# Last batch of a two-layer kernel's first attention: its normalization ahead of the next layer's rows, and the pieces woven into that layer's first group moved by one step

## What is computed

```
x = x + L0_xattn(layernorm(x), ctx)     # latent attention, per batch
x = x + L0_ffn(layernorm(x))            # gated feed-forward in 8-bit floats
x = x + L1_xattn(layernorm(x), ctx, ctx)
x = x + L1_ffn(layernorm(x))            # top-2 of 8 experts
# L0_xattn, for one batch
p   = softmax(theta(ctx) @ phi(x))
t_x = p @ g(x)                          # 128 x 512 per batch
h   = relu((t_x - mean(t_x)) * rsqrt(var(t_x) + eps) * gamma + beta)   # mean and var over ALL of t_x
out = out_w @ h + out_b + ctx
# L0_ffn
out = q(gelu(q(x) @ q(w0)) * (q(x) @ q(w1))) @ q(w_linear)
```

## Time and profile before

| | us |
|---|---|
| median of 3 runs (837.96 to 839.0) | 838.62 |
| the profiled execution | 841.42 |
| its span (first to last instruction) | 839.7 |
| busy in the span: PE | 744.5 |
| DVE | 578.2 |
| ACT | 398.3 |
| POOL | 354.9 |

### The profile page before, as it was taken

How to read it: one execution, slowest core, us unless ns; L and a number is a source line. 1 busy time by engine, 2 the same in 40 slices (tenths; PEclk the granted TensorE clock), 3 DMA queues, 4 the chain that set the end, 5 groups by cost and what they waited for, 6 DMA issues and landing times. The chain is left out here.

```text
span 839.7 us, 14278 instructions
## 1 busy us (share of the span) xinstructions
PE 744.5 (89%) x4265; PEld 307.2 (37%) x4265; DVE 578.2 (69%) x1100; ACT 398.3 (47%) x744; POOL 354.9 (42%) x344
## 2 busy tenths in 40 slices
PE   4999997989999999798999899999971699999993
PEld 2344443444444443121222222222231355555551
DVE  4688888585858587668988988976746255555551
ACT  2534543553636372476777667746750222222220
POOL 4654454012020212536576587565465033333332
PEclk9999999999999999799999999968995799999998
DMA  8999740018181775333434453434343589889974
GB/s 307 352 133 257 275 185 0 1 36 303 36 297 71 271 255 183 76 94 84 103 100 103 100 167 94 110 102 119 99 146 142 90 111 131 123 135 120 121 103 62
DMA packets 114166, 117.51 MB, mean 140 GB/s; under 512 B 54824, under 2 KB 78248, under 8 KB 113840
## 3 DMA queue, kind: packets, MB, share of 16 engines
q1 hardware_dynamic: 102992, 94.48, 40.4%
q0 software_dynamic: 10384, 22.02, 15.4%
q10 hardware_dynamic: 720, 0.13, 0.1%
HBM read 43.61 MB, written 59.56 MB: 123 GB/s over the span
## 5 line engine op out<-in xcount | busy, mean ns | idle before, releaser
L1422 ACT ACTIVATE t_room<-l_b 128x512 f32<-128x512 f32 x256 | 139.3, 594 | 53.6 <-PE l_b L1317 47.8
L1930 POOL DMA_INDIRECT out<-ex_y,t_tag x39 | 61.6, 1581 | 123.9 <-DMA out<-ex_y,t_tag 63.7
L1826 PE MATMUL ex_hp<-w1h,h_stack 128*128 x312 | 78.1, 320 | 17.2 <-DVE ex_hl L1879 16.7
L1495 DVE TENSOR_REDUCE l_negm<-l_a 128x2 f32<-128x1024 f32 x64 | 75.2, 1220 | 16.6 <-PE l_a L1262 16.6
L1846 PE MATMUL ex_yp<-w2h,ex_ht 128*128 (+1 forms) x234 | 76.2, 380 | 5.2 <-DVE ex_ht L1890 4.5
L1495 DVE TENSOR_REDUCE h_negm<-l_a 128x2 f32<-128x1024 f32 x56 | 66.0, 1221 | 17.9 <-PE l_a L1262 17.9
L1865 ACT ACTIVATE ex_hf<-ex_pre 128x352 f32<-128x352 f32 x39 | 19.4, 497 | 118.2 <-DVE ex_pre L1885 118.2
L1328 PE MATMUL l_pv<-t_room,l_vt 128*32 128x512 f32 x512 | 73.1, 645 | 0.1
L1336 PE MATMUL l_sm<-t_room,ones_f 128*32 128x512 f32 x512 | 70.3, 623 | 0.0
L806 PE MATMUL ps_st<-f_xt,wg 128*128 128x512 fp8e4 x256 | 65.7, 379 | 3.4 <-ACT f_y L857 1.8
L806 PE MATMUL ps_r<-f_xt,wg 128*128 128x512 fp8e4 x256 | 65.7, 379 | 0.0
(11 more groups left out here) (247 smaller groups left out, 1482.2 us busy)
## 6 DMA issues: line engine op xcount, KB each, us to landing
slots_x<-empty SPq DMA_DIRECT2D x8, 2376.0 KB, 11.1
slots_x<-empty SPq DMA_DIRECT2D x7, 2112.0 KB, 16.1
h_stack<-h_parts SPq DMA_DIRECT2D x96, 64.0 KB
l_stack<-l_parts SPq DMA_DIRECT2D x96, 64.0 KB
f_stage<-in_w SPq DMA_DIRECT2D x8, 704.0 KB, 7.2
w1l<-in_ctx SPq DMA_DIRECT2D x8, 512.0 KB, 8.3
f_stage<-in_w SPq DMA_DIRECT2D x8, 512.0 KB
h_kf<-in_ctx SPq DMA_DIRECT2D x16, 256.0 KB, 3.1
```

The costliest lines, as they stand in the source:

```text
L1422: act.activation(weights_at(u, c, h)[:, :], B[t % 2][:, :], ACT.Exp, scale=SCALE).then_inc(b_ok, 1)
L1495: dve.tensor_reduce(negm[u % 2][:, 2 * half:2 * half + 2, j], A[half][:, :, :], AX.X, ALU.max, negate=True)\
L1826: mm = pe.matmul(HP[i % 2][:, 0:H], xt[i % AHEAD][:, xp * FC + f, :], w1p[wp][:, bass.ds(e, 1), f * H:(f + 1) * H], start=k == 0, stop=k = ...
L1930: pool.indirect_dma_start(out=out, out_offset=bass.IndirectOffsetOnAxis(ap=tags[i % TAGS][:, 0:1].bitcast(U32), axis=0), in_=y[i % YS][:, ...
```

## The change

Two edits, no instruction added or removed.

1. In the last attention step, DVE's `G.normal_rows(dve, X, 0, ...)` moves from ahead of `normalized(dve, 7)` to behind it.
2. In the first feed-forward group, PE's `variance_of(7)` moves from the end of step 3 to step 4, `mean_of(8)` from 10 to 11 and `variance_of(8)` from 12 to 13. DVE's `spread_of(8)` moves from the end of step 9, where it stood behind `added(7)`, to the end of step 8.

```
             if m == 1:
                 pe.wait_ge(sr_ok, B)
                 mean_of(pe, B - 1)
-            if m == 3:
+            if m == 4:
                 variance_of(pe, B - 1)
...
-            if m == 10:
+            if m == 11:
                 mean_of(pe, B)
-            if m == 12:
+            if m == 13:
                 variance_of(pe, B)
...
                 if more:
                     normal_rows(i + 1)
-                else:
-                    G.normal_rows(dve, X, 0, range(G.G))
                 if back:
                     normalized(dve, i)
                 if more:
                     low_x(i + 1, 1 - par)
                 else:
+                    G.normal_rows(dve, X, 0, range(G.G))
                     G.widen(dve, 0)
...
             if m == 5:
                 shifted(dve, B - 1)
+            if m == 8:
+                spread_of(dve, B)
             if m == 9:
                 added(dve, B - 1, A)
-                spread_of(dve, B)
```

## The result

The changed kernel takes 826.9 us (median of 4 runs, 824.71 to 834.83) against 838.29 for the kernel before beside it: ratio 0.9869, 95% interval 0.9825 to 0.9913. The forecast was 829.8 with a range from 827.8. The edited stretch came out as forecast, within half a microsecond; the rest came from another place and is the subject of the experiments.

A forecast was written before the change was run, and what follows sets the result against it. PE was taken to bound the kernel, standing still at the handover and waiting in the first feed-forward group; 4.7 + 4.2 = 8.9, taken as 8.8 us, gave 829.8 us from the median 838.62, range 827.8 to 834.0.

The forecast's parts named there:

- What bounds the kernel: Stretch from 137 to 205 us: PE stands still at the handover and waits three times in the first feed-forward group.
- The handover, 4.7 us: From batch 6's output product to batch 8's transposes: normalizing batch 7 earlier starts the transposes at 146.1 against 150.78.
- The first group, 4.2 us: First feed-forward group: moving the small matmuls and statistics removes PE's three waits, 1.22 + 2.31 + 0.63 us.
- All three waits: PE's idle before three small attention matmuls in the first feed-forward group: 1.05, 2.14 and 0.46 us.
- DVE keeps up: First group: DVE gains only 3.43 us, yet its last cast comes 0.6 us before PE's sixteenth linear-weight product needs it.
- the clock falls in the new hole: Rival at the handover: PE's clock drops before the transposes, costing 0.9 to 1.8 us; chance 0.14 together with pacing.
- the pacing: Handover: POOL's additions set the row tiles' speed, freeing DVE at 143.5, at worst 144.45; chance 0.14 with the clock.
- The sum: Both parts of the edited stretch: 4.7 + 4.2 = 8.9 us, taken as 8.8; chance of both in full 0.62.
- the clock in the second attention: Rival "Slower": more low PE clock in second attention and experts; 17.6 us more costs 8.8 us; 842 us, chance 0.03.
- the forecast's 0.9895: Whole kernel: ratio expected in the repeats if the change is worth only its own stretch, 8.8 us.

The follow-up runs named there:

- the third: Third profile of the kernel before, unchanged and run once more for its profile: one run of 842.0 us.
- the repeats: The whole change run twice more against the kernel before: 820.26 against 828.77 us, ratio 0.9899; then 830.2 us, ratio 0.9882.

## Why the prediction missed its range while its steps held

- **What bounds the kernel.** Right: PE's chain bounds this stretch, and as its waits went, all behind it came earlier.
- **The handover, 4.7 us.** Measured 4.39 to the transposes. The value products start at once and run at full clock; the `added` of batch 6 is the new late one. The over-estimate of 0.3 is in the row tiles: I let them free DVE 3.7 us after their start; they took 4.08. The order was as foretold: the first tile is through (0.78 us) soon after the second addition starts, the next two (1.49 each) come out behind the second and third. But that third addition ends 6.03 us after L434 starts, in before 5.66 (141.32 + 1.32 - 136.98), as the first two took 3.02 us instead of 2.67; the widening starts at 142.54, in the old times 143.78, for which the prediction had taken 143.5, with 143.9 for an addition held up by DVE. That POOL paces the tiles was shown by holding POOL back. The Trainium skill, GPSIMD Engine Reference, section 1 (Specifications), counts two-input operations of DVE among those that contend, too. This case agrees from POOL's side: the delay is all in the first addition, which lies beside L442 and L447 and takes 1.61 us also where no other addition follows it, against 1.27 for the next. L442, the one with two inputs in SBUF, kept its 0.69. An `added` (L455), which like L447 reads one bank and one tile in SBUF, lies beside that addition of 1.27 us, so L442 is the likelier cause; no run separates the two.
- **The first group, 4.2 us.** Measured 4.45. All three waits went, each for its forecast reason. The extra 0.25 is a thing I left out: a small matmul that has waited holds PE 0.24 us until the next product, one that has not 0.14, three times.
- **DVE keeps up.** Right, with 0.55 us of slack for a forecast 0.6.
- **Rival "the clock falls in the new hole".** I gave it, with the pacing, 0.14, arguing from a 2.14 us wait across which the clock stayed. That argument fell: of four profiles with this hole two show the fall, two not. Its price was 0.7 us each time, not 0.9 to 1.8. The old hole's price also varies: the value products took 5.20 us to the next start in the profile before, 6.54 in the third.
- **The sum.** Per stretch 8.83 us in the first profile; over three profiles each, before 68.30, 68.30 and 69.64, after 59.47, 60.18 (137.61 to 197.79) and 59.46 (136.27 to 195.73): 9.0 us on average for a forecast of 8.8.
- **The step that failed** is the term that the sum does not have: what lies behind 205 us was taken as unchanged, and the range, 827.8 to 834.0, was drawn from the edited stretch alone. In the first pair of profiles that part gave 3.6 us. Behind this stands the sentence "Three runs within 1.04 us of each other speak against a schedule that depends on luck". Three runs on one chip said nothing of the rest: the same program took 828.8, 836.0 and 839.9 us on three chips (medians, each chip at another time), 832.5 to 839.5 on one of them, and the first comparison of four runs had the changed kernel from 824.7 to 834.8. I had even named the place, the clock in the second attention, but only as a way to become slower; it works both ways. The first comparison found 11.4 us, with an interval that holds the forecast's 0.9895; the repeats found 8.5 and 9.7. The 8.8 rests on steps that the profiles bear out; that the first median fell below the range looks like chance, since both repeats came out less and no run ties the rest to the edits.

What stays open: why the same program is 11 us slower on one chip than on another. The median granted clocks there, 0.959, 0.956 and 0.953, stand for 11 us more at the lower level from the first to the last, so for half of it; the other half is not accounted for, nor why the clock differs. No experiment here touched those stages.

## What to carry to other kernels

In lists of fixed order a tiny instruction that waits holds up everything behind it, and on the engine that bounds the stretch its whole wait is paid: put it one step later than its operand's worst time, then look whether the producer can keep up without the echo (its own waits that followed from that one). When a move frees one engine, ask for the next releaser in its list (here the operation that frees the banks) and for what shares memory with the moved work; both could be read off the profile before. And measure what the untouched rest of the program varies by, on more than one chip, before the edge of a range is put within a microsecond.

## What the runs showed of the hardware that was not expected

- Four 128x512 f32 to 8-bit `tensor_scalar` operations on DVE took 4.05 us beside POOL additions of the same size, 2.14 us with all but the first addition held back. The other way, a POOL addition took 2.22 us beside a 128x2048 widening on DVE (which kept its 1.23) and 1.27 us with that on ACT.
- A PE hole of 2.2 us behind 3.5 us and more of unbroken work was followed by the lower clock in two profiles of four; holes of 0.3 and 0.9 us in one each were not.
- Two executions of one program were 12.4 us apart in a span of 840, of which 8.5 us go back to 17 us more at the lower level in an 85 us stretch (0.88 against 0.98). A third was 13.0 us longer than the shortest with 0.96 in that stretch, and its clock over the whole span stands for only 7.4 us.
- With POOL held back, its first addition, beside DVE's L442 and L447, took 1.61 us, its second, beside an `added`, 1.27.
